# Two slot regions in the second of four mixture-of-experts layers, and the next layer's keys made at another place

## The reference

```
for k in range(2):
    y = dispatch_compute(xf, top_experts[:, k], w1, w2, capacity=256)
    out = out + y * expert_weights[:, k][:, None]
```

## Time and profile before

| | us |
|---|---|
| median of 3 runs | 713.46 (713.31 to 714.85) |
| the profiled execution, its own time | 709.9 |
| its span in the trace | 708.2 |
| PE busy | 567.8 (80%) |
| DVE busy | 405.1 (57%) |
| ACT busy | 293.9 (41%) |
| POOL busy | 293.7 (41%) |

### The profile page before, as it was taken

How to read it: one execution, slowest core, us unless ns; L and a number is a source line. 1 busy time by engine, 2 the same in 40 slices (tenths; PEclk the granted TensorE clock), 3 DMA queues, 4 the chain that set the end, 5 groups by cost and what they waited for, 6 DMA issues and landing times.

```text
span 708.2 us, 13280 instructions
## 1 busy us (share of the span) xinstructions
PE 567.8 (80%) x3758; PEld 456.0 (64%) x3758; DVE 405.1 (57%) x1637; ACT 293.9 (41%) x732; POOL 293.7 (41%) x354
## 2 busy tenths in 40 slices
PE   5788779799848988239995899978899998954991
PEld 3466556699815666229993465754799846744991
DVE  3676655688757666402224876635488776653443
ACT  3455532244424564214441655532244335432660
POOL 3112567266610127634552110576166611272551
PEclk9999859999977897559997999759999997556996
DMA  8990012233181001112215000012123140012214
GB/s 270 225 420 5 24 34 62 75 87 86 57 292 65 2 8 40 37 50 61 68 55 155 13 1 2 31 42 80 44 85 91 52 119 1 0 45 76 64 48 127
DMA packets 56182, 54.84 MB, mean 77 GB/s; under 512 B 8200, under 2 KB 50976, under 8 KB 55056
## 3 DMA queue, kind: packets, MB, share of 16 engines
q1 hardware_dynamic: 48272, 39.75, 18.9%
q0 software_dynamic: 7840, 14.25, 6.2%
HBM read 34.99 MB, written 20.86 MB: 79 GB/s over the span
## 4 chain that ended last, share of the span: by engine, by line
PE 54%; DVE 12%; issue 10%; POOL 8%; ACT 5%; DVEq 5%; DMA 4%; SPq 0%; POOLq 0%; ACTq 0%
PE bank L861 17%; PE bank L873 11%; POOL slots L554 6%; PE bank L698 5%; PE bank L685 4%; DVE x L1530 3%; PE bank L849 2%; ACT pay L953 2%; DVE stat L1120 2%; PE bank L816 2%; PE bank L647 2%; PE bank L818 2%; PE bank L833 2%; DMA slots<-pay,pos 1%; PE bank L659 1%
## 5 line engine op out<-in xcount | busy, mean ns | idle before, releaser
L580 POOL DMA_INDIRECT result<-xn,row x133 | 131.6, 989 | 132.2 <-DVE row L1480 122.1
L554 POOL DMA_INDIRECT slots<-pay,pos x112 | 110.9, 990 | 57.4 <-issue 34.0
L517 POOL TENSOR_TENSOR rstd<-spread,minus_half 128x4 f32<-128x4 f32 (+1 forms) x33 | 34.2, 1036 | 207.2 <-DVE spread L1113 174.9
L861 PE MATMUL bank<-xnT,gat 128*128 128x128 f32 x808 | 111.1, 282 | 1.1 <-DVE gat L1489 1.1
L873 PE MATMUL bank<-w,hsh 128*128 (+1 forms) x752 | 106.1, 276 | 1.7 <-DVE hsh L1496 1.1
L861 PEld LDWEIGHTS bank<-xnT,gat 128*128 128x128 f32 x808 | 100.7, 196 | 2.5 <-ACT xnT L1046 1.3
L873 PEld LDWEIGHTS bank<-w,hsh 128*128 128x128 f32 x752 | 94.6, 192 | 2.4 <-issue 2.4
L698 PEld LDWEIGHTS bank<-vblk,probT 128*128 128x128 f32 x384 | 52.5, 207 | 37.3 <-ACT probT L993 25.9
L698 PE MATMUL bank<-vblk,probT 128*128 128x36 f32 x384 | 54.3, 290 | 14.1 <-ACT probT L993 11.1
L1046 ACT COPY xnT<-bank 128x128 f32<-128x128 f32 x133 | 35.6, 269 | 64.8 <-PE bank L849 59.8
L1507 DVE COPY xn<-bank 128x128 f32<-128x128 f32 x110 | 31.4, 285 | 50.4 <-PE bank L873 50.4
(11 more groups left out here) (233 smaller groups left out, 1042.1 us busy)
## 6 DMA issues: line engine op xcount, KB each, us to landing
xg<-slots SPq DMA_DIRECT2D x133, 64.5 KB
w<-in_w SPq DMA_DIRECT2D x4, 2048.0 KB, 11.8
pay<-result SPq DMA_DIRECT2D x21, 256.0 KB, 4.2
w<-in_w SPq DMA_DIRECT2D x1, 2560.0 KB, 19.0
w<-in_w SPq DMA_DIRECT2D x1, 2304.0 KB, 14.1
result<-xn,row POOLq DMA_INDIRECT x133, 2.2
slots<-zeros SPq DMA_DIRECT2D x1, 2064.0 KB, 25.8
slots<-pay,pos POOLq DMA_INDIRECT x112, 2.3
```

The lines of the kernel that those rows point to most:

```text
L517: own(pool.tensor_tensor(rstd[:, lo:hi], spread[:, lo:hi], minus_half[:, lo:hi], ALU.pow))
L554: pool.indirect_dma_start(out=(slots1 if l == 1 else slots)[:, :], out_offset=bass.IndirectOffsetOnAxis(ap=pos[:, t, k:k + 1], axis=0), in ...
L580: pool.indirect_dma_start(out=result[:, :], out_offset=bass.IndirectOffsetOnAxis(ap=row[:, s % TURN:s % TURN + 1], axis=0), in_=ysb[:, s % ...
L861: last = pe.matmul(bank[2 + p][:, c * P:(c + 1) * P], weights[:, c * P:(c + 1) * P], xgT[:, p, :], start=True, stop=True)
```

## The change

Four things are changed, all in layer 1.

- The slots are two DRAM arrays, `slots1[0]` for first choices and `slots1[1]` for second ones, of 2048 rows each (8 experts x 256). Zeroing takes two DMAs where it took one. A token's place is now 256 times its expert plus its rank in either array.
- The 32 expert tiles go through all first choices (16 tiles, two for each expert) and then through all second ones. SP waits for the 16 scatters of first choices before tile 0 and for the 16 of second choices, on a semaphore of their own, before tile 16.
- POOL scatters the second choices of groups 2 and 3 behind the first choices of group 3 (steps 24.5 to 26).
- `next_context` of layer 1 leaves step 18 and stands behind the walk: on PE behind the last ranks, on ACT between the exponential and the gelu table, on DVE behind `counts`.

```
+SECOND = E * CAP // P
-        slots1 = nc.dram_tensor("slots1", [SEG * CAP, ROW], F32, kind="Internal").ap()
+        slots1 = [nc.dram_tensor(f"slots1_{k}", [E * CAP, ROW], F32, kind="Internal").ap() for k in range(2)]
...
-                   scale_r=8, tokens_r=10, logits=10, pick=11, ranks=11, scatter=11, place=12, next_context=18),
+                   scale_r=8, tokens_r=10, logits=10, pick=11, ranks=11, scatter=11, place=12),
...
-                    e[s] = s // RING if engine[1] == 1 else numbers(engine[0], tab_e, s, 1, E - 1)[0]
+                    e[s] = s % SECOND // (CAP // P) if engine[1] == 1 else numbers(engine[0], tab_e, s, 1, E - 1)[0]
...
-            sp.dma_start(slots1.rearrange("(t p) d -> p t d", p=P),
-                         zeros[:].unsqueeze(1).to_broadcast([P, SEG * CAP // P, ROW])).then_inc(zero_done, 16)
+            for k in range(2):
+                sp.dma_start(slots1[k].rearrange("(t p) d -> p t d", p=P),
+                             zeros[:].unsqueeze(1).to_broadcast([P, E * CAP // P, ROW])).then_inc(zero_done, 16)
...
-                sp.wait_ge(scat[l], 16 * TOPK[l] * NTILE)
+                sp.wait_ge(scat[l], 16 * (1 if l == 1 else TOPK[l]) * NTILE)
...
+                    src = slots1[s // SECOND][r:r + P, :] if l == 1 else slots[bass.ds(r, P), :]
...
-                        return [(first + i) * P for i in range(n)]
+                        return [(first + i) % SECOND * P for i in range(n)]
...
+                    if l == 1 and s == SECOND:
+                        sp.wait_ge(scat_second, 16 * NTILE)
...
-            pool.iota(limit[:], [[CAP, 2], [2 * CAP, E]], base=CAP, channel_multiplier=0, allow_small_or_imprecise_dtypes=True)
+            pool.iota(limit[:], [[0, 2], [CAP, E]], base=CAP, channel_multiplier=0, allow_small_or_imprecise_dtypes=True)
-            pool.iota(row_base[1][:], [[CAP // P, 2], [2 * CAP // P, E]], base=0, channel_multiplier=0,
                      allow_small_or_imprecise_dtypes=True)
+            pool.iota(row_base[1][:], [[0, 2], [CAP // P, E]], base=0, channel_multiplier=0,
                      allow_small_or_imprecise_dtypes=True)
...
-                            out=(slots1 if l == 1 else slots)[:, :],
+                            out=(slots1[k] if l == 1 else slots)[:, :],
...
-                            bounds_check=(SEG * CAP if l == 1 else E * REGION) - 1, oob_is_err=False).then_inc(scat[l], 16)
+                            bounds_check=(E * CAP if l == 1 else E * REGION) - 1,
+                            oob_is_err=False).then_inc(scat_second if l == 1 and k == 1 else scat[l], 16)
...
-                    *[(at["scatter"] + 2 * k + half, GROUPS, scatter_rows(k, half))
-                      for k in range(TOPK[l]) for half in range(2)]])
+                    *[(at["scatter"] + 2 * k + half, GROUPS if l != 1 or k == 0 else GROUPS[:2], scatter_rows(k, half))
+                      for k in range(TOPK[l]) for half in range(2)],
+                    *([(at["scatter"] + at_last, (g,), scatter_rows(1, half))
+                       for g, half, at_last in ((2, 0, 5.5), (2, 1, 6), (3, 0, 2.5), (3, 1, 3))] if l == 1 else [])])
...
                 pe.wait_ge(ld_w[l], 16 * (4 if l == 3 else 2))
+                if l == 1:
+                    next_context(l, 0)
...
                     exp_logits(l)
+                if l == 1:
+                    next_context(l, 0)
+                if l in (1, 3):
                     preload(ACT.Gelu_apprx_tanh if l == 1 else ACT.Gelu)
...
                 rest_of_parts(l, shared, TABLES, 1)
+                if l == 1:
+                    next_context(l, 0)
                 experts(l)
...
-                    dve.tensor_tensor(valid[:, 0:n].rearrange("p (e k j) -> p e k j", e=E, k=2),
-                                      count[:].rearrange("p (k e) -> p e k", k=2).unsqueeze(3).to_broadcast([P, E, 2, CAP // P]),
+                    dve.tensor_tensor(valid[:, 0:n].rearrange("p (s j) -> p s j", s=SEG),
+                                      count[:].unsqueeze(2).to_broadcast([P, SEG, CAP // P]),
```

More of the change, by code:

```diff
@@ L246, in flamingo @@
         scat = [sem(f"scat{l}") for l in range(LAYERS)]
+        scat_second = sem("scat_second")
         padded = sem("padded")
@@ L395, in _ @@
             for l in range(LAYERS):
-                src = slots1 if l == 1 else slots
                 if l != 1:
@@ L404, in _ @@
                 else:
-                    sp.wait_ge(zero_done, 16)
-                sp.wait_ge(scat[l], 16 * TOPK[l] * NTILE)
+                    sp.wait_ge(zero_done, 16 * 2)
+                sp.wait_ge(scat[l], 16 * (1 if l == 1 else TOPK[l]) * NTILE)
                 sp.wait_ge(Z["m_tab"], l + 1)
@@ L416, in load @@
                         sp.wait_ge(Z["t_id"], s + (base - RING + 1))
-                    sp.dma_start(xg[:, q, :], src[bass.ds(r, P), :]).then_inc(filled[q], 16)
+                    src = slots1[s // SECOND][r:r + P, :] if l == 1 else slots[bass.ds(r, P), :]
+                    sp.dma_start(xg[:, q, :], src).then_inc(filled[q], 16)
                 def starts(first, n):
                     if l == 1:
-                        return [(first + i) * P for i in range(n)]
+                        return [(first + i) % SECOND * P for i in range(n)]
                     return numbers(mybir.EngineType.SP, tab_r, first, n, E * REGION - P)
@@ L551, in scatter @@
                     if l == 1 and g == 0 and k == half == 0:
-                        pool.wait_ge(zero_done, 16)
+                        pool.wait_ge(zero_done, 16 * 2)
                     for t in range(g * GT + half * GT // 2, g * GT + (half + 1) * GT // 2):
                         pool.indirect_dma_start(
-                            out=(slots1 if l == 1 else slots)[:, :],
+                            out=(slots1[k] if l == 1 else slots)[:, :],
                             out_offset=bass.IndirectOffsetOnAxis(ap=pos[:, t, k:k + 1], axis=0),
                             in_=pay[:, k, t, :], in_offset=None,
-                            bounds_check=(SEG * CAP if l == 1 else E * REGION) - 1, oob_is_err=False).then_inc(scat[l], 16)
+                            bounds_check=(E * CAP if l == 1 else E * REGION) - 1,
+                            oob_is_err=False).then_inc(scat_second if l == 1 and k == 1 else scat[l], 16)
                 return scatter
@@ L894, in _ @@
                        (at["context_nT"], (0,), context_nT)] if l == 0 else []),
-                    (at["next_context"] if l < 3 else 0, (0,) if l < 3 else (), next_context),
+                    (at.get("next_context", 0), (0,) if "next_context" in at else (), next_context),
                     (at["tokens"], GROUPS, transpose_tokens),
@@ L1365, in counts @@
                     n = TILES[1]
-                    dve.tensor_tensor(valid[:, 0:n].rearrange("p (e k j) -> p e k j", e=E, k=2),
-                                      count[:].rearrange("p (k e) -> p e k", k=2).unsqueeze(3).to_broadcast([P, E, 2, CAP // P]),
-                                      seg_at[:].rearrange("p (e k j) -> p e k j", e=E, k=2), ALU.is_gt)
+                    dve.tensor_tensor(valid[:, 0:n].rearrange("p (s j) -> p s j", s=SEG),
+                                      count[:].unsqueeze(2).to_broadcast([P, SEG, CAP // P]),
+                                      seg_at[:].rearrange("p (s j) -> p s j", s=SEG), ALU.is_gt)
                     dve.drain()
```

## The result

| | before | after |
|---|---|---|
| median, us | 713.31 (9 runs, 710.4 to 725.7) | 706.25 (9 runs, 705.4 to 710.0) |
| ratio | | 0.9912, 95% interval 0.9896 to 0.9927 |
| profiled execution, its span | 709.9, 708.2 | 707.4, 705.5 |

What follows compares the result with a forecast made beforehand. POOL's scatter queue ahead of layer 1's experts was taken as the bound. Reordering gains 7.6 us, all other terms 0: 713.46 - 7.6 = 705.9 us, range 703.9 to 709.4.

Steps and rivals of the forecast that it cites:

- What bounds: End of layer 1's routing: the experts wait for POOL's queue of scatters, 12.3 us longer than for routing itself.
- two limits in turn: POOL's queue holds group 3's root behind group 1's eight scatters, then group 3's first choices among sixteen scatters in a row.
- Term 1: POOL's order ahead of layer 1's experts: group 3's fourth first choice starts at 301.17, 7.6 us earlier; tile 0 at 305.4.
- 2.5 or more: Sign of being right: POOL idle about 2.5 us or more ahead of group 3's first scatter in layer 1.
- Term 2: Eight second-choice scatters moved back on POOL: tile 0's result 1 us late, but copies and SP's wait unaffected; cost 0.
- Term 3: Layer 2's keys behind layer 1's walk: 5.4 us on DVE, ending 2.9 us ahead of tile 0; no direct gain, cost 0.
- The two unknowns: Before tile 0: whether key products slow POOL's scatters, and whether shared DMA engines delay landings and first load; each taken as 0.
- Keys against scatters: DVE's key products may slow POOL's scatters: gain 0 to 1.0 us, loss 0 to 1.5, cancelling within 0.5; taken as 0.
- the old pair: Two scatters beside DVE's keys ahead of group 3's root, 1.46 and 1.50 us in place of 0.97, together 1.02 more.
- Shared DMA engines: Second choices beside the last first-choice landing and first slot loads: bounds 0 to 2.0 us, taken as 0.
- Zeroing: Zeroing the slots in two DMAs instead of one: cost 0.
- PE starts tile 0 from idle at the lower clock as before; taken as unchanged: Start of layer 1's experts: eight products in 2.08 us against 1.06 at tile 3, taken as unchanged.

Runs made afterwards that it cites:

- e4: Kernel before with two slot regions and first-choice tiles first, but POOL's old queue order and layer 2's keys at step 18: 711.78 us, ratio to before 0.9986.
- e2: Changed kernel with layer 2's keys left at step 18: 706.90 us, ratio to the kernel before 0.9871.
- e5: Changed kernel with all sixteen second-choice scatters of layer 1 behind all first choices on POOL: 709.96 us, ratio to the kernel before 0.9947.
- e3: Kernel before with only layer 2's keys moved behind the walk: 716.15 us, ratio to the kernel before 1.0018.
- e7: Changed kernel without DVE's four layer 2 key products, so its result differs: run once, 713.09 us.
- e6: Changed kernel with DVE's four layer 2 key products made twice, same values written again: run once, 703.39 us.
- e1: Changed kernel with both slot regions in one array of 4096 rows, zeroed by one DMA: 706.86 us.
- again: Changed kernel unchanged, run once more for a second profile: 705.48 us, ratio to the kernel before 0.9862.
- v3: Changed kernel with group 3's root ahead of group 1's second choices on POOL and its transposes in bank 0: 703.65 us, ratio to before 0.9876.

## Why the prediction was right, by its steps

- **What bounds.** POOL's queue, by two limits in turn. Shown: e4 shortens the row by four scatters and brings tile 0 forward by 4.85 of the 5.1 us expected, e2 adds the order and gets 7.65.
- **Term 1.** Root to places: 10.31 (forecast 10.30). Places to first scatter: 300.91 - 300.14 = 0.77 (0.79). First to fourth: 4.32 (3.92; a scatter of 1.36 in it). Fourth to PE: 4.45 (4.22). The root came 1.03 earlier, since the two long scatters ahead of it were short again; the range had allowed for it. Tile 0: 1.03 - 0.40 - 0.23 makes 0.4 more than the forecast 7.6, 8.0 us earlier. POOL stood idle for 4.28 us ahead of group 3's first scatter, where I asked for 2.5 or more.
- **Term 2.** Cost 0 for the copies and for SP; e5 shows that with sixteen it isn't. Tile 0's result was scattered at 36.85, 7.0 us after PE's start, 0.8 late (forecast 1).
- **Term 3.** 5.24 us from 300.83 to 306.07, 3.5 ahead of the slots. The statement that the move gives nothing by itself held to 0.36 us. It holds only in the new order: with the old queue the same move brings tile 0 forward by 1.77 (e3), since there sixteen scatters start behind group 2's places.
- **The two unknowns.** Keys against scatters: both halves happened, 1.03 given back and 0.39 lost, where I had them cancel; e2 keeps about half a us of the old pair and lands at 30.18. The Trainium skill (SBUF — State Buffer, "Who interferes with whom") infers that `tensor_tensor` leaves descriptor generation alone; e7 against e6 doesn't fit it for one early scatter, 0.39 us longer, and agrees for the later ones. But a scatter here also reads its places (`pos`) from SBUF, and by the first half of the rule, that on reads, this may be what waits; no run tells the two apart. Shared DMA engines, taken as 0: the first load took 2.1 in place of 1.80, and fourth scatter to PE cost 0.2 more.
- **Zeroing.** Taken as 0, which no row of before could show. e1 did: one DMA in place of two gave 706.86 against 705.48 and group 1's first scatter at 279.19, inside the range of the traces with two (274.5 to 279.9).
- **The term that was off.** "PE starts tile 0 from idle at the lower clock as before; taken as unchanged". From tile 0 to the transpose of tile 3 it was 317.88 - 312.99 = 4.89 before and 315.03 - 309.68 = 5.35 after, since the second tile's first products took 1.73 us, where they had 1.27: the clock rose later (granted 0.84 from 316 to 317 before, 0.51 from 313 to 314 after). From tile 0 to the layer's end it is 64.76 to 65.07 in three profiles, 64.30 in the one of before. But this is not shown to be the change's doing: e3, with the old queue, took 5.87 from tile 0 to tile 3 and 65.29 to the end, and e5, with a new one, 4.87 to tile 3. Of what the layer gained, 7.2 to 7.55 us, the forecast's 7.6 had 0.4 too little ahead of the loop and took 0 for 0.5 to 0.8 lost in it. That the two nearly cancel is luck, of about half a us; the 8 us ahead of the loop are not.
- **The whole time.** 7.1 by the medians, 6.3 by the ratio. The later layers take back little: from layer 1's last result to layer 2's first it is 131.99 to 132.35 in the three profiles, 131.87 before, and from there to the end of the span 198.5 to 199.1 against 199.0. The whole times alone would not carry the account: e3 and e4 gain in the layer and hardly or not in the time.

## What to carry to other kernels

When one engine's queue stands on the chain, ask of each entry who needs it first, and put what is needed last behind; what you gain is bounded by the next wait that was hidden in the queue, here the places of the last group, and then the root in front of them. The entries put behind are free as long as the ring buffers after them have slack, which can be counted ahead from one timeline: eight cost nothing here, sixteen stopped PE for 4.48 us. Compare two profiles from an event next to the change, since executions of one kernel drift by several us before they get there.

## What was not expected of the hardware

- Group 1's first scatter stood between 274.5 and 279.9 in traces whose work up to there is the same but for the zeroing, with the granted clock of the window 30 to 60 between 0.77 and 0.95.
- Four products of 128x512 on DVE with both inputs in SBUF lengthened one or two of the scatters that started in their first 2 us from 0.97 to between 1.36 and 1.50 us, and none of those that started later; in layer 0 they lengthened none.
- The first load of slots took 2.1 to 2.2 us beside scatters of second choices (after, again, v3), and 1.8 and 1.9 without them (before, e3).
- One pause of PE of 4.48 us (e5) was followed by a granted clock of 0.51 for 2 us and products of 1.71 and 1.91 us in place of 1.06.
